# A metaformer block: the expert layer from all eight experts per token to sorted tiles of the two chosen ones

## The chip, the cores and the metric

The kernel runs on one core of a Trainium2 chip. The metric is the time of one execution on the device in microseconds (us). A core has five engines with a queue of instructions each: TensorE (PE, matmuls; its weight loads are listed as PEld), VectorE (DVE), ScalarE (ACT), GpSimd (POOL) and SyncE (SP, which here only issues transfers). They signal each other by semaphores. Results of PE go to PSUM, here eight banks of 128 partitions x 512 float32 numbers, and everything else is in SBUF.

## The reference

An image tensor of 8 x 64 x 16 x 16 passes four stages: a deformable convolution, an LSTM over the 256 positions, a second deformable convolution, and a layer of experts. The change is in the last. There are 2048 tokens of 64 channels, 8 experts with 682 hidden numbers each, and each token's result uses its two most probable experts:

```python
logits = flat @ router_w.T
probs = jax.nn.softmax(logits, axis=-1)
topk_probs, topk_idx = jax.lax.top_k(probs, TOP_K)          # TOP_K = 2
topk_probs = topk_probs / (jnp.sum(topk_probs, axis=-1, keepdims=True) + 1e-09)
onehot = jax.nn.one_hot(topk_idx, N_EXPERTS, dtype=flat.dtype)
gates = jnp.einsum('nk,nke->ne', topk_probs, onehot)
h1 = jnp.einsum('nc,ehc->neh', flat, w1)
h3 = jnp.einsum('nc,ehc->neh', flat, w3)
h = jax.nn.silu(h1) * h3
y = jnp.einsum('neh,ech->nec', h, w2)
out = jnp.einsum('ne,nec->nc', gates, y)
```

`flat` is the layer-normalised input; `out` is added to the input.

## The kernel before

The program is written out engine by engine, and the order of each engine's instructions is the order of the code; nothing is scheduled. Between the engines stand waits on semaphores (`wait_ge`).

**Number format.** Where float32 accuracy is wanted at the speed of float16 matmuls, a number is held as a float16 high part and a float16 rest. The tokens stand as `xp`, with the high parts of 64 channels on 64 partitions and the rests on the other 64, so that one matmul with 128 rows takes both. Weights have a high and a rest matrix (`wh`, `wl`; in `w2p` the two are side by side).

**Weights.** They are loaded at the start (L277, L279). During the LSTM, a serial chain of 256 steps, DVE takes the largest absolute value in 56 pieces (`largest_part`, L1201) and then ACT and DVE split the weights into the two parts in pieces of 256 columns (`high_part` L814, `low_part` L1239). Only two of the four pairs of experts fit beside the originals; the other two are stored and fetched again (L290, L296).

**Expert layer.** After the last layer norm PE makes the logits (L588). DVE computes the gates in a chain of small operations (L1388 to L1415), each of which waits for the one before. ACT and POOL split the tokens (L917 to L1000). Then a loop with two passes over 88 units runs, 176 units in all. A unit is 128 hidden rows of a pair of experts for 512 tokens:

- PE, `first` (L604, L605): four matmuls 128x512, for h1 and h3 with the two parts of the weights.
- ACT: SiLU of h1 (L932). DVE: the product with h3 into `hid` (L1443). ACT: the high part `hh` (L928). POOL: the rest `hl` (L1007).
- PE, `second` (L619), three units later: eight matmuls 128x128 with `hh` and `hl` as the stationary side; in 16 of the units they are 256 columns wide.
- DVE, `gather` (L1427): after eleven units the results of 512 tokens are multiplied by the gates and added to `acc`.

After the loop DVE adds the halves (L1454), PE transposes (L634), DVE adds to the input (L1458), SP stores the output (L301).

Of the kernel before, what the change touches and what calls it, by code (L numbers as in the profile page):

```python
# [22 lines left out]
I32 = mybir.dt.int32  # L23
ALU = mybir.AluOpType
# [4 lines left out]
T = H * W  # L29
# [34 lines left out]
SPLIT = (POWER + 16, POWER + 30 + 2 * PAIRK)  # L64
# [7 lines left out]
MLAG = 3  # L72
MR = 4
# [5 lines left out]
NCH = 4  # L79
CH = B * T // NCH  # L80
JJ = CH // 128

def build(nc, x, consts, conv_w, conv_b, sample_w, bn, lstm_u, lstm_v, lstm_b, router, w13, w2, out):
    with ExitStack() as ctx:
# [6 lines left out]
        bank = [ctx.enter_context(nc.psum_tensor(f"bank{i}", [P, 512], F32)) for i in range(8)]  # L92
# [54 lines left out]
        w13s = sb("w13s", [P, PAIRS, 2 * PH])  # L147
        wh = [sb(f"wh{q}", [P, 2 * PH], F16) for q in range(2)]
        wl = [sb(f"wl{q}", [P, 2 * PH], F16) for q in range(2)]
        w2f = sb("w2f", [P, PAIRS, W2B, C])  # L150
        w2p = [sb(f"w2p{q}", [P, W2B, 2, C], F16) for q in range(2)]
        hid = sb("hid", [P, MR, 512])

        def over(t, at, shape, dt=F32):
# [14 lines left out]
        xp = over(st0, 0, [P, 2 * COLS], F16)  # L170
        silu = over(st0, 1024, [P, 1024]).rearrange("p (u n) -> p u n", u=2)
        acc = over(st1, 0, [P, 2048]).rearrange("p (j h n) -> p j h n", j=8, h=2)
        slo = hid[:, 0:SR // 2, :].rearrange("p a b -> p (a b)").bitcast(F16) \
            .rearrange("p (s k n) -> p s k n", s=SR, k=TG)
        hh = zw[0][:, :, :, :, :].rearrange("p a b c d -> p (a b c d)")[:, 0:MR * 512] \
            .rearrange("p (u n) -> p u n", u=MR)
        hl = zw[1][:, :, :, :, :].rearrange("p a b c d -> p (a b c d)")[:, 0:MR * 512] \
            .rearrange("p (u n) -> p u n", u=MR)
        gt = xc[:, :].rearrange("p (k g e) -> p k g e", k=8, e=E)
        small = spare[:, 0:128].rearrange("p (k g) -> p k g", k=8)  # L180
        g1 = spare[:, 128:256].rearrange("p (j h e) -> p j h e", j=8, h=2)
        ge = spare[:, 256:320].rearrange("p (q j h k) -> p q j h k", q=2, j=8, h=2)
# [17 lines left out]
        for l in range(4):  # L200
            for n in ("mean", "xc", "sq", "var", "sd", "rs", "rb", "rt", "xn"):
                if l != 2 or n not in ("rs", "rb", "rt"):
                    s(f"n{l}_{n}")
        for n in ("ld_const", "ld_mean", "ld_x", "ld_conv", "ld_lstm", "ld_w13", "ld_late", "ld_w2",
                  "zero", "bn_a", "bn_d",
                  "c_max", "c_tr", "c_pow", "c_bc", "c_scale",
                  "w_part", "w_max", "w_tr", "w_pow", "w_bc", "w_scale", "w_fac", "w_high", "w_split", "w_stored", "l_scaled",
                  "l_gi", "l_o", "l_act", "l_oact", "l_c", "l_tc", "l_h", "l_hc", "l_up", "l_res", "l_init", "l_zero", "r_half", "r_seed", "r_newton",
                  "e_pads", "e_conv", "e_om", "e_turn", "e_omt", "e_sig", "e_dist", "e_far", "e_tents", "e_tent",
                  "m_w0", "m_w1", "m_high", "m_scaled", "m_parts", "m_log", "m_max", "m_exp", "m_sm", "m_ge",  # L210
                  "m_h", "m_silu", "m_hid", "m_hh", "m_hl", "m_zero", "m_y", "m_acc", "m_sum", "m_tr",
# [3 lines left out]

# [36 lines left out]

        block = ctx.enter_context(nc.Block())
# [3 lines left out]
        def _(sp):  # L258
# [16 lines left out]
            for e in range(PAIRS):  # L275
                for hf in range(2):
                    sp.dma_start(w13s[hf * C:hf * C + C, e, :], w13[e]).then_inc(s("ld_w13"), 16)  # L277
            for e in range(PAIRS):
                sp.dma_start(w2f[:, e, :, :], w2[e]).then_inc(s("ld_w2"), 16)  # L279

            def parts(q):
                kept = w13s[:, 2 + q, :].bitcast(F16).rearrange("p (k n) -> p k n", k=2)
                kept2 = w2f[:, 2 + q, :, :].rearrange("p a c -> p (a c)").bitcast(F16)
                used2 = w2p[q][:, :, :, :].rearrange("p a k c -> p (a k c)")
                return ((kept[:, 0, :], wh[q][:, :]), (kept[:, 1, :], wl[q][:, :]), (kept2, used2))

            for q in range(2):
                sp.wait_ge(s("w_split"), q + 1)
                for kept, used in parts(q):
# [1250 lines left out]
```

## Time and profile before

| | us |
|---|---|
| three runs of the kernel | 954.67, 957.54, 958.70; median 957.54 |
| span of the profiled execution, first to last instruction | 952.8 |
| LSTM, 145.7 to 559.4 | 413.7 |
| second convolution, to about 670 | 110 |
| layer norm, router and token split, to 689.3 | 19 |
| expert loop, 689.3 to 943.4 | 254.1 |
| tail, to 952.8 | 9.4 |

The profiled execution has no time of its own beside its span; the span is 4.7 us under the median of the runs. The table of slices of the page has each engine's busy share in fortieths of the span. The expert loop is slices 29 to 39: there PE has mostly 9, ACT and POOL 8, DVE 6 and 7, and TensorE's granted clock stands at 9. A span of an instruction goes from its start to its modelled end; since matmuls are pipelined, the distance from one start to the next says what a matmul costs its engine.

### The profile page before, as it was taken

The page shows a single profiled execution, that of the slowest core. Times are in us where ns is not written, and L with a number is a line of the kernel's source. Part 1 is how long each engine was busy: PE and PEld are TensorE (multiplying, and loading weights), DVE is VectorE, ACT ScalarE, POOL GpSimd, SP SyncE. Part 2 cuts the span into 40 slices and gives each one's busy share as a digit, 9 for nine tenths or more (in the row PEclk, how much of TensorE's full clock was granted, in tenths as well). Part 3 has the DMA queues.
Part 4 walks back from the last instruction along what each step waited for, and adds up shares of the span by engine and source line. Part 5 has one row for each costly group of instructions (what it writes and reads, how often), then busy time and mean ns, then how long its engine had stood idle before and what let it go on. Part 6 is the DMA issues. An engine that isn't in the chain of part 4 may idle for free.

```text
span 952.8 us, 18695 instructions
## 1 busy us (share of the span) xinstructions
PE 800.3 (84%) x6356; PEld 594.2 (62%) x6356; DVE 570.5 (60%) x1752; ACT 556.2 (58%) x1664; POOL 366.6 (38%) x297
## 2 busy tenths in 40 slices
PE   5899987777777776789988768999689999899995
PEld 3587875555655555566666547889446666466663
DVE  3888854556456466334344346887457667467765
ACT  3676752333355365334444355777478888588884
POOL 0878620000000000003000007874268888588884
PEclk7999995555555555555555556999689999899998
DMA  9700000000001100000000000000000100200001
GB/s 224 175 2 1 2 1 1 1 1 1 0 1 78 78 1 1 1 0 1 1 1 1 1 1 1 2 1 2 1 1 2 59 21 2 80 1 2 2 1 23
DMA packets 5860, 18.54 MB, mean 19 GB/s; under 512 B 1093, under 2 KB 2822, under 8 KB 5254
## 3 DMA queue, kind: packets, MB, share of 16 engines
q1 hardware_dynamic: 5478, 17.21, 6.2%
q8 instruction: 52, 0.85, 0.4%
q14 instruction: 42, 0.34, 0.1%
q10 hardware_dynamic: 288, 0.13, 0.1%
HBM read 9.47 MB, written 0.52 MB: 10 GB/s over the span
## 4 chain that ended last, share of the span: by engine, by line
PE 41%; POOL 22%; DVE 13%; issue 11%; ACT 11%; DVEq 1%; POOLq 1%; DMA 0%; SPq 0%; ACTq 0%
POOL zw L1007 21%; PE bank L558 10%; PE bank L383 6%; PE bank L560 6%; PE bank L400 6%; DVE bank L1320 5%; PE bank L348 4%; DVE hr L1324 4%; ACT bank L885 4%; ACT bank L889 4%; PE bank L524 2%; PE bank L370 1%; DVE hid L1089 1%; PE bank L315 1%; PE bank L413 1%
## 5 line engine op out<-in xcount | busy, mean ns | idle before, releaser
L1007 POOL TENSOR_TENSOR zw<-hid,zw 128x512 f16<-128x512 f32 x176 | 203.9, 1159 | 49.3 <-ACT zw L928 38.9
L558 PE MATMUL bank<-hr,lv 64*64 64x8 f32 x512 | 97.0, 261 | 98.8 <-DVE hr L1324 98.4
L966 POOL TENSOR_TENSOR st<-tent,tentx 128x768 f32<-128x768 f32 x72 | 112.2, 1589 | 173.3 <-DVE tentx L1081 123.8
L1443 DVE SCALAR_TENSOR_TENSOR hid<-bank,wsc,st 128x512 f32<-128x512 f32 x176 | 131.9, 750 | 76.0 <-ACT st L932 70.1
L558 PEld LDWEIGHTS bank<-hr,lv 64*64 64x64 f32 x512 | 72.8, 201 | 158.4 <-DVE hr L1324 158.2
L885 ACT ACTIVATE bank<-bank 64x16 f32<-64x16 f32 x256 | 39.2, 153 | 196.8 <-PE bank L560 196.5
L604 PE MATMUL bank<-st,wh 128*128 128x512 f16 x352 | 136.9, 389 | 11.5 <-POOL st L1000 5.4
L932 ACT ACTIVATE st<-bank,wsc 128x512 f32<-128x512 f32 x176 | 120.9, 687 | 39.8 <-PE bank L605 22.0
L605 PE MATMUL bank<-st,wl 128*128 128x512 f16 x352 | 136.8, 389 | 0.0
L966 POOL TENSOR_TENSOR st<-sq 128x768 f32<-128x768 f32 x9 | 13.2, 1498 | 309.3 <-DVE sq L1309 308.5
L1320 DVE TENSOR_TENSOR_SCAN bank<-bank,scan_add 64x24 f32<-64x24 f32 x256 | 52.9, 207 | 127.8 <-ACT bank L885 127.5
L619 PEld LDWEIGHTS bank<-w2p,zw 128*128 128x128 f16 x1408 | 96.8, 98 | 45.4 <-POOL zw L1007 4.1
L619 PE MATMUL bank<-w2p,zw 128*128 128x128 f16 (+1 forms) x1408 | 114.2, 224 | 3.0 <-POOL zw L1007 3.0
L717 ACT ACTIVATE shi<-bank 128x512 f16<-128x512 f32 x144 | 85.4, 596 | 52.2 <-PE bank L383 51.0
L1089 DVE SCALAR_TENSOR_TENSOR hid<-bank,shi 128x512 f16<-128x512 f32 x144 | 96.1, 686 | 31.0 <-ACT shi L717 29.8
L928 ACT CAST zw<-hid 128x512 f16<-128x512 f32 x176 | 106.9, 608 | 4.1 <-DVE hid L1443 4.1
L383 PE MATMUL bank<-ident,st 128*128 128x128 f32 x576 | 91.7, 283 | 1.7 <-DVE hid L1089 1.4
L560 PE MATMUL bank<-hr,lv 64*64 64x8 f32 x512 | 91.6, 251 | 0.0
L562 PE MATMUL bank<-hr,lv 64*64 64x8 f32 x512 | 91.6, 251 | 0.0
L560 PEld LDWEIGHTS bank<-hr,lv 64*64 64x64 f32 x512 | 84.7, 224 | 0.0
L562 PEld LDWEIGHTS bank<-hr,lv 64*64 64x64 f32 x512 | 84.4, 223 | 0.0
L1324 DVE SCALAR_TENSOR_TENSOR hr<-tog,bank 64x8 f32<-64x8 f32 x256 | 39.4, 154 | 72.7 <-ACT bank L889 72.7
(184 smaller groups left out, 1340.4 us busy)
## 6 DMA issues: line engine op xcount, KB each, us to landing
w13s<-w SPq DMA_DIRECT2D x8, 704.0 KB, 17.9
w2f<-w SPq DMA_DIRECT2D x4, 384.0 KB, 25.4
w13s<-wh SPq DMA_DIRECT2D x2, 704.0 KB, 3.7
w13s<-wl SPq DMA_DIRECT2D x2, 704.0 KB, 5.0
wh<-w13s SPq DMA_DIRECT2D x2, 704.0 KB, 3.9
wl<-w13s SPq DMA_DIRECT2D x2, 704.0 KB, 5.1
w2f<-w2p SPq DMA_DIRECT2D x2, 384.0 KB, 4.9
w2p<-w2f SPq DMA_DIRECT2D x2, 384.0 KB, 5.7
```

The source lines that it names most:

```text
L383: mm = nc.tensor.transpose(bank[3 + g % RING][:, k * 128:k * 128 + 128], st[m % 2][:, t, tap, half * 128:half * 128 + 128], ident[:, :])
L558: nc.tensor.matmul(both[:, 0, t, :], lv[:, C:2 * C], prev, start=False, stop=True, skip_group_check=True)
L560: nc.tensor.matmul(both[:, 1, t, :], lv[:, 0:C], prev, start=False, stop=True, skip_group_check=True).then_inc(s("l_gi"), 1)
L562: nc.tensor.matmul(go, lv[:, 2 * C:3 * C], prev, start=False, stop=True, skip_group_check=True).then_inc(s("l_o"), 1)
L604: nc.tensor.matmul(bk[:, :], wh[q][:, col:col + 128], xp[:, tok], start=True, stop=False)
L605: nc.tensor.matmul(bk[:, :], wl[q][:, col:col + 128], xp[:, tok], start=False, stop=True)\
L619: mm = nc.tensor.matmul(bank[4 + 2 * (g % 2) + j // 2][:, lo:lo + n], part[:, u % MR, j * 128:j * 128 + 128], rhs, start=(t == 0 and j % 2 ...
L928: nc.scalar.copy(hh[:, u % MR, :], hid[:, u % MR, :]).then_inc(s("m_hh"), 1)
L932: nc.scalar.activation(silu[:, u % 2, :], bank[u % 2][:, :], ACT.Silu, scale=wsc[:, 4:5])\
L966: nc.gpsimd.tensor_tensor(st[p][:, t, k:k + KG, :].rearrange("p k (y x) -> p k y x", x=16), ty, tx, ALU.mult)\
L1007: nc.gpsimd.tensor_tensor(hl[:, u % MR, :], hid[:, u % MR, :], hh[:, u % MR, :], ALU.subtract)\
L1443: nc.vector.scalar_tensor_tensor(out=hid[:, u % MR, :], in0=bank[2 + u % 2][:, :], scalar=wsc[:, 5:6], in1=silu[:, u % 2, :], op0=ALU.mult ...
```

## The change

Only the chosen experts are computed. The 4096 pairs of a token and an expert are sorted by expert, and each expert's pairs are padded to tiles of 128. With 8 experts, 39 tiles hold every possible outcome, and the program always runs 39.

1. **Routing** (DVE, L1537 to L1591). The two best experts are found from the logits; a scan over each partition's tokens and two matmuls with constant matrices (`ones_p`, `upper`, L672, L673) give each pair its place in the sorted order; 33 comparisons build two selection matrices (`tsel`, `lsel`), and 32 matmuls (L679) turn them into a list of tokens by tile and lane. From it come `xidx` (what to fetch), `yidx` (where results go) and `etab` (the expert of each tile). The gates are computed after that.
2. **Tokens** are transposed (L666), split by ACT and POOL and written to memory by one transfer (`xrows`, L364).
3. **Tiles.** For each tile POOL issues an indirect transfer that fetches 128 rows of 256 bytes (L1157), PE transposes them (L692), ACT copies them (`xts`), PE does `first` with the tokens as the stationary side and the weights as the moving side, 341 columns at a time (L705). ACT takes SiLU of 682 columns, DVE the product, PE transposes the product in six blocks (L716), ACT makes the high part, DVE the rest, and PE does `second` (L729) with 12 matmuls of 128 columns. DVE adds the two halves of the result (L1627), and POOL issues an indirect transfer that spreads the 128 rows in memory (L1164).
4. **Weight addresses.** PE loads the tile's expert from `etab` into a register (L685) and computes the addresses of the weights from it. All weights now stay in SBUF in both parts; the stores and fetches L290 and L296 go away, and the loads are 52 transfers in place of 12. The split during the LSTM has 64 pieces of at most 228 columns in place of 56 of 256.
5. **Tail.** SP waits for all the spread rows, reads them back in two transfers (L369), and DVE multiplies by the gates and adds.

The core of the diff:

```diff
-W13K = 2 * PAIRS * PH // CHUNK
-W2K = PAIRS * W2B * C // CHUNK
-PAIRK = 2 * PH // CHUNK + W2B * C // CHUNK
+W13K = 44
+W2K = 12
+HCUT = [0, 228, 456, 684, 912, 1140, EW]
+PAIRK = 16
+TILE = 128
+NT = (2 * B * T + E * (TILE - 1)) // TILE
+AHEAD = 4
...
@@ tensor
-                        nc.tensor.matmul(bk[:, :], wh[q][:, col:col + 128], xp[:, tok], start=True, stop=False)
-                        nc.tensor.matmul(bk[:, :], wl[q][:, col:col + 128], xp[:, tok], start=False, stop=True)\
...
+            def expert(t):
+                return pe.value_load(etab[0:1, t:t + 1], min_val=0, max_val=E - 1)
+            def turn_tokens(t):
+                pe.wait_ge(s(f"m_g{t % AHEAD}"), 16 * (t // AHEAD + 1))
+                if t > 0:
+                    pe.wait_ge(s("m_xts"), t)
+                nc.tensor.transpose(bank[4][:, 0:64].bitcast(F16), xg[:, t, :], ident16[:, :])\
+                    .then_inc(s("m_xtp"), 1)
+            def first(t, e):
+                n = HID // 2
+                pe.wait_ge(s("m_xts"), t + 1)
+                for m in range(2):
+                    if t > 0:
+                        pe.wait_ge(s(("m_silu", "m_hid")[m]), t)
+                    for half in range(2):
+                        for part in range(2):
+                            at = 2 * SLOT + part * EW + m * HID + half * n
+                            mm = nc.tensor.matmul(duo[m][:, half * 512:half * 512 + n], xts[:, t % 3, :],
+                                                  w16[:, bass.ds(e * SLOT + at, n)],
+                                                  start=(part == 0), stop=(part == 1))
+                    mm.then_inc(s("m_h"), 1)
+            def turn_hidden(t):
+                pe.wait_ge(s("m_hid"), t + 1)
+                for b in range(EB):
+                    if t > 0 and b % 4 == 0:
+                        pe.wait_ge(s("m_hl"), 2 * t - 1 + b // 4)
+                    mm = nc.tensor.transpose(bank[6 + b // 4][:, b % 4 * 128:b % 4 * 128 + 128],
+                                             htok[:, t % 2, b * 128:b * 128 + 128], ident[:, :])
...
+            for t in range(NT + 2):
+                if t < NT:
+                    first(t, owners[t])
+                    if t + 1 < NT:
+                        owners.append(expert(t + 1))
+                        turn_tokens(t + 1)
+                if 1 <= t <= NT:
+                    turn_hidden(t - 1)
+                if t >= 2:
+                    second(t - 2, owners[t - 2])
@@ gpsimd
-                    nc.gpsimd.tensor_tensor(hl[:, u % MR, :], hid[:, u % MR, :], hh[:, u % MR, :], ALU.subtract)\
-                        .then_inc(s("m_hl"), 1)
+            def fetch(t):
+                if t >= AHEAD:
+                    gp.wait_ge(s("m_xtp"), t - AHEAD + 1)
+                gp.indirect_dma_start(xg[:, t, :], None, xrows[:, :],
+                                      bass.IndirectOffsetOnAxis(ap=xidx[:, t:t + 1], axis=0))\
+                    .then_inc(s(f"m_g{t % AHEAD}"), 16)
+            def spread(t):
+                gp.wait_ge(s("m_ys"), t + 1)
+                gp.indirect_dma_start(yrows[:, :], bass.IndirectOffsetOnAxis(ap=yidx[:, t:t + 1], axis=0),
+                                      ybuf[:, t, :], None).then_inc(s("m_rows"), 16)
+            for t in range(AHEAD):
+                fetch(t)
+            gp.wait_ge(s("m_idx"), 2)
+            for t in range(NT):
+                if t + AHEAD < NT:
+                    fetch(t + AHEAD)
+                spread(t)
@@ vector
+            for t in range(NT + 2):
+                if t < NT:
+                    gated(t)
+                if 1 <= t <= NT:
+                    low(t - 1)
+                if t >= 2:
+                    rows_out(t - 2)
```

PE's queue in the middle of the expert loop before, one unit, with what each instruction waits for (names are those of the tensors; `st` holds the tokens `xp`, `zw` the parts `hh` and `hl`):

```order
L600 REGISTER_ALU
L604 MATMUL bank<-st,wh 128x512 [waits m_hid]
L605 MATMUL bank<-st,wl 128x512
L604 MATMUL bank<-st,wh 128x512
L605 MATMUL bank<-st,wl 128x512
L619 MATMUL bank<-w2p,zw 128x128 [waits m_hl]
L619 MATMUL bank<-w2p,zw 128x128 x7
```

And now, in a tile, from the last matmul of `first` (`st` holds the rows `xg` and `xts`, `hid` the product `htok`, `w2s` the weights of `second`; ISA is a register instruction):

```order
L705 MATMUL duo<-w13s,st 128x341
L685 TENSOR_LOAD etab
L685 ISA x2
L692 MATMUL bank<-ident,st 128x128 [waits m_xts,m_g0]
L716 MATMUL bank<-ident,hid 128x128 [waits m_hl,m_hid]
L716 MATMUL bank<-ident,hid 128x128 x3
L716 MATMUL bank<-ident,hid 128x128 [waits m_hl]
L716 MATMUL bank<-ident,hid 128x128
L729 ISA [waits m_hl,m_ys]
L729 MATMUL bank<-w2s,zw 128x128 x2
```

Each pair of matmuls of `second` and each matmul of `first` has a register instruction ahead of it, and the transposition of the next tile's rows, which waits for a transfer (`m_g0`), stands ahead of the hidden transpositions of the tile before.

POOL's queue at the start of the expert loop before:

```order
L990 MEMSET st 128x2048 [waits c1_out_ps]
L1000 TENSOR_TENSOR st<-sq,st 64x1024 [waits m_scaled,m_high,m_zero]
L1000 TENSOR_TENSOR st<-sq,st 64x1024 [waits m_parts,m_scaled,m_high]
L1004 UNCONDITIONAL_BRANCH [waits m_parts]
L1004 ISA
L1007 TENSOR_TENSOR zw<-hid,zw 128x512 [waits m_hh]
```

And now:

```order
L1143 MEMSET hid 128x2x86 [waits c1_sz_done,c1_out_ps]
L1148 TENSOR_TENSOR st<-sq,st 128x8x64 [waits m_high] x2
L1157 DMA st<-xrows,xidx 128x128 [waits m_idx,m_xrow]
L1157 DMA st<-xrows,xidx 128x128 x3
L1157 DMA st<-xrows,xidx 128x128 [waits m_xtp,m_idx]
L1164 DMA yrows<-st,yidx 9216x64 [waits m_ys]
L1157 DMA st<-xrows,xidx 128x128 [waits m_xtp]
```

POOL no longer computes in the loop; it issues a fetch and a spread for each tile, in turn, and the spread of tile t (which waits for its result, `m_ys`) stands ahead of the fetch of tile t + 5.

## Rows read from the trace of the kernel before

**Rows 1.** The page's chain that ended last, by engine and by line.
```profile
PE 41%; POOL 22%; DVE 13%; issue 11%; ACT 11%; DVEq 1%; POOLq 1%; DMA 0%; SPq 0%; ACTq 0%
POOL zw L1007 21%; PE bank L558 10%; PE bank L383 6%; PE bank L560 6%; PE bank L400 6%; DVE bank L1320 5%; PE bank L348 4%; DVE hr L1324 4%; ACT bank L885 4%; ACT bank L889 4%; PE bank L524 2%; PE bank L370 1%; DVE hid L1089 1%; PE bank L315 1%; PE bank L413 1%
```
**Rows 2.** Stages: start:end, length, busy us by engine, clock, DMA share, GB/s.
```profile
145.70:559.40 413.70, 314.85 (x1969) 244.63 (x1968) 206.30 (x1101) 174.12 (x937) 8.84 (x6) 0.50 0.03 10
680.00:695.00 15.00, 7.53 (x26) 4.54 (x25) 10.38 (x27) 6.13 (x7) 4.23 (x2) 0.50 0.00 0
689.30:943.36 254.06, 244.75 (x2112) 153.62 (x2112) 167.72 (x317) 210.60 (x352) 203.86 (x176) 0.97 0.04 16
```
**Rows 3.** Groups of instructions in 700 to 800: busy us, mean ns, idle before.
```profile
L1007 POOL TENSOR_TENSOR zw<-hid,zw 128x512 f16<-128x512 f32 x75 | 86.9, 1159 | 14.4 <-ACT zw L928 9.8
L1443 DVE SCALAR_TENSOR_TENSOR hid<-bank,wsc,st 128x512 f32<-128x512 f32 x75 | 56.3, 750 | 32.8 <-ACT st L932 31.5 <-issue 0.4
L932 ACT ACTIVATE st<-bank,wsc 128x512 f32<-128x512 f32 x75 | 51.5, 687 | 11.3 <-PE bank L605 3.5
L928 ACT CAST zw<-hid 128x512 f16<-128x512 f32 x74 | 45.0, 607 | 0.0
```
**Rows 4.** Timeline, PE, one unit: start, duration, instruction.
```profile
703.36 0.38 PE L604 MATMUL bank<-st,wh 128*128 128x512 f16 x1
...
704.22 0.61 PE L619 MATMUL bank<-w2p,zw 128*128 128x128 f16 x8
...
704.67 0.38 PE L604 MATMUL bank<-st,wh 128*128 128x512 f16 x1
```
**Rows 5.** Timeline of the second convolution: transposes, and what reads them.
```profile
663.19 0.60 PE L383 MATMUL bank<-ident,st 128*128 128x128 f32 x4
...
663.58 0.69 DVE L1089 SCALAR_TENSOR_TENSOR hid<-bank,shi 128x512 f16<-128x512 f32 x1 [0.20 <-ACT shi L717]
663.63 0.22 PE L400 MATMUL bank<-zw,shi 128*128 128x128 f16 x1
```
**Rows 6.** Router: one row of the timeline, then groups by shape.
```profile
683.98 0.29 DVE L1388 TENSOR_REDUCE spare<-bank 128x16 f32<-128x128 f32 x1 [2.83 <-PE bank L588]
...
L1396 DVE TENSOR_TENSOR xc<-xc,spare 128x128 f32<-128x128 f32 x1 | 1.9, 1932 | 0.0
L1415 DVE TENSOR_SCALAR spare<-spare,wsc 128x128 f32<-128x128 f32 x1 | 0.3, 286 | 0.0
L1407 DVE SCALAR_TENSOR_TENSOR spare<-spare 128x16 f32<-128x16 f32 x1 | 0.2, 174 | 0.0
L1000 POOL TENSOR_TENSOR st<-sq,st 64x1024 f16<-64x1024 f32 x2 | 4.2, 2116 | 12.0 <-ACT sq L920 11.8 <-POOL st L1000 0.2
```
**Rows 7.** Transfers: issues, KB each, median us from issue to landing; one issue.
```profile
xs<-x SPq DMA_DIRECT2D x2, 256.0 KB, 4.5
out<-xs SPq DMA_DIRECT2D x4, 128.0 KB, 2.5
mean_w<-consts ACTq DMA_DIRECT2D x1, 64.0 KB, 1.9
...
5.09 0.43 SPq L269 DMA_DIRECT2D convw<-conv_w  x1
```
**Rows 8.** The chain in order of time: POOL's queue between two units.
```profile
937.20 0.03 POOLq L1006
```
**Rows 9.** Timeline, DVE, two LSTM steps with a piece of the split.
```profile
275.05 0.21 DVE L1320 TENSOR_TENSOR_SCAN bank<-bank,scan_add 64x24 f32<-64x24 f32 x1 [0.22 <-ACT bank L885]
...
275.95 0.47 DVE L1239 SCALAR_TENSOR_TENSOR wl<-w13s,wsc,wh 128x256 f16<-128x256 f32 x1
276.64 0.21 DVE L1320 TENSOR_TENSOR_SCAN bank<-bank,scan_add 64x24 f32<-64x24 f32 x1 [0.22 <-ACT bank L885]
```
**Rows 10.** Timeline of the tail.
```profile
943.36 2.29 DVE L1427 SCALAR_TENSOR_TENSOR st<-bank,spare,st 128x128 f32<-128x128 f32 x8 [3.21 <-PE bank L619]
...
947.12 1.29 DVE L1458 TENSOR_TENSOR xs<-xs,bank 128x512 f32<-128x512 f32 x2 [0.15 <-PE bank L634]
```

More of the change, by code:

```diff
@@ L184, in place @@
+        tiles, ends, start_c = [rk[:, 8 * k:8 * k + 8] for k in range(3)]
+        spot, away, tile_n, lane, gate = [rk[:, 32 * k:32 * k + 32].rearrange("p (k g) -> p k g", k=2)
+                                          for k in range(1, 6)]
+        bits = rk[:, 192:192 + NP40 // 2].bitcast(F16)
+        raw = rk[:, 224:224 + NP40].bitcast(I32)
+        passed = spare[0:1, 0:NP40 * E].rearrange("p (t e) -> p t e", e=E)
+        owner = rk[0:1, 264:264 + NP40]
         def place(p, g):
@@ new lines, in _ @@
+            for j in range(8):
+                mm = nc.tensor.transpose(bank[4 + j // 4][:, j % 4 * 128:j % 4 * 128 + 128],
+                                         xn[:, j * 128:j * 128 + 128], ident[:, :])
+                if j % 4 == 3:
+                    mm.then_inc(s("m_xps"), 1)
+            pe.wait_ge(s("m_rank"), 1)
+            last = counts[:, :, 15]
+            nc.tensor.matmul(bank[7][:, 0:E], ones_p[:, :], last, start=True, stop=True, skip_group_check=True)
+            nc.tensor.matmul(bank[7][:, E:2 * E], upper[:, :], last, start=False, stop=True, skip_group_check=True)\
+                .then_inc(s("m_tot"), 1)
@@ new lines, in _ @@
+            pe.wait_ge(s("m_tsel"), 1)
+            for c in range(32):
+                if c % 8 == 0:
+                    pe.wait_ge(s("m_lane"), c // 8 + 1)
+                mm = nc.tensor.matmul(bank[7][:, 64:64 + NP40], lsel[:, c, :], tsel[:, c, :],
+                                      start=(c == 0), stop=(c == 31), skip_group_check=True)
+            mm.then_inc(s("m_code"), 1)
+            def expert(t):
+                return pe.value_load(etab[0:1, t:t + 1], min_val=0, max_val=E - 1)
@@ new lines, in second @@
+            def second(t, e):
+                if t > 0:
+                    pe.wait_ge(s("m_ys"), t)
+                for b in range(EB):
+                    if b % 4 == 0:
+                        pe.wait_ge(s("m_hl"), 2 * t + 1 + b // 4)
+                    for part in (hh, hl):
+                        mm = nc.tensor.matmul(bank[5][:, 0:2 * C],
+                                              part[:, t % 3, b * 128:b * 128 + 128],
+                                              w216[:, bass.ds(e * HP + (2 * HP + b * 128), 128)],
+                                              start=(b == 0 and part is hh), stop=(b == EB - 1 and part is hl),
+                                              skip_group_check=True)
+                mm.then_inc(s("m_y"), 1)
@@ L903, in _ @@
                     early_tents(image_step(n, 12))
-                for part in range(2):
-                    if SPLIT[part] <= n < SPLIT[part] + 2 * PAIRK:
-                        high_part(2 * PAIRK * part + n - SPLIT[part])
+                if split_piece(n) is not None:
+                    high_part(split_piece(n))
             act.wait_ge(s("l_h"), STEPS + 1)
@@ L939, in _ @@
+            turned_tokens(0)
+            for t in range(NT + 1):
+                if t < NT:
+                    gated(t)
+                if t + 1 < NT:
+                    turned_tokens(t + 1)
+                if t > 0:
+                    high(t - 1)
         @block.gpsimd
@@ L1002, in _ @@
[L1002 to L1008 removed]
+            gp.wait_ge(s("c1_sz_done"), NG * B)
+            nc.gpsimd.memset(htok[:, :, HID:HP], 0.0).then_inc(s("m_zero"), 1)
@@ new lines, in _ @@
+            for c in range(32):
+                k, g = c // 16, c % 16
+                ins = nc.vector.tensor_scalar(lsel[:, c, :], lane_c[:, :], lane[:, k, g:g + 1], code_v[:, c:c + 1],
+                                              ALU.is_equal, ALU.mult)
+                if c % 8 == 7:
+                    ins.then_inc(s("m_lane"), 1)
+            note(nc.vector.tensor_tensor(passed, tile_c[0:1, :].unsqueeze(2).broadcast_to([1, NP40, E]),
+                                         ends[0:1, :].unsqueeze(1).broadcast_to([1, NP40, E]), ALU.is_ge))
```

517 lines of the change are left out of this document (281 added, 236 removed).

## The prediction

> **What bounds the kernel now.** I read the page's chain first: the loop's POOL instruction (L1007) alone is 21% of the span, the largest line [rows 1]. Then the table by stages. The expert loop takes 254.1 of 952.8 us; in it PE is busy 244.8 and POOL 203.9 us, at a granted clock of 0.97, that is, at the 2.4 GHz level nearly throughout [rows 2]. Then the groups within the loop and one unit of the timeline. A 512-column matmul costs PE 0.215 us (four from 703.36 to 704.22) and one of 128 columns 0.056 (eight from 704.22 to 704.67), so a unit is 1.31 us of gapless PE [rows 4]; POOL needs 1.16 and 0.15 between two [rows 3]. The loop is bound by PE and POOL at once: 176 x 1.31 = 231 us, the rest being wide units, the turn of the loop and the start. The LSTM (413.7 us) and the convolutions are not touched but for the pieces of the weight split.
>
> **What goes.** The whole loop and, ahead of it, POOL's two passes over `xp` (L1000, 2.12 us each) [rows 6]. The weight stores and fetches ran beside other work and give nothing.
>
> **The LSTM.** 64 pieces in place of 56, each a little smaller. A step with a DVE piece of 0.47 us goes from 275.05 to 276.64, 1.59 us, with DVE idle 0.22 before the next scan [rows 9]: the piece lies in DVE's slack. Cost 0; without that cover, 8 x 0.47 = 4 us. The 52 loads are issued at 0.43 us each [rows 7], 22 us, under the first convolution, and are needed only in the LSTM: 0.
>
> **Work in a tile.** PE by the rows above: eight matmuls of 341 columns at 0.143 (0.215 x 341/512) = 1.14, one transpose 0.06, six float32 transposes at 0.11 (663.19 to 663.63 for four [rows 5]) = 0.66, twelve of 128 columns = 0.67; together 2.5 us. 39 tiles are 99 us of PE against 231: not a quarter, since tokens are padded and the hidden numbers must be transposed. DVE: product of 682 columns 0.95 (0.75 for 512 [rows 3], with the 1.2 ns per column between it and the 0.29 for 128 columns [rows 6]), rests of 512 and 256 columns 0.69 and 0.42 (0.69 [rows 5]), sum of 128 columns 0.29; 2.35. ACT: SiLU 0.9 (0.69 x 682/512), high parts 0.61 and 0.35, tokens 0.3; 2.2 [rows 3]. POOL: two issues, 2P.
>
> **What a tile costs.** No engine is full at these numbers, so I look for the chain that closes on itself. Call P POOL's time for one indirect issue and L the time from its end to landing. The result of tile t is summed (`m_ys`); POOL issues its spread (P), then the fetch of tile t+5 (P), which lands after L. PE transposes that fetch in the middle of tile t+4, and behind it, in order, stand the six transposes of tile t+3 and `second` of t+2, whose sum closes the ring two tiles further on. From the landing: transposes 0.06 + 0.60, `hh` 0.61, `hl` 0.69 + 0.42, last four matmuls of `second` with the tail of the last 0.39, sum 0.29: 3.1 us. So two tiles take 2P + L + 3.1. A second ring needs no transfer: product of tile t starts, PE's transposes, `hh`, both `hl`, sum, next product: 0.66 + 0.61 + 1.11 + 0.29 = 2.7 us.
>
> P is not in this trace. Below, SP's issue of a plain transfer: 0.43 [rows 7]. Above, the longest POOL instruction here over 128 or 64 partitions, 2.12 [rows 6]. I take 1.2, near the pass over 128 partitions (1.16 [rows 3]), since 128 rows must be addressed. L: the smallest timed transfer lands 1.9 after the start of its issue, so 1.5 after its end; the longest row here is 4.5 [rows 7]. A fetch is 32 KB: I take 2.0. Then T = (2.4 + 2.0 + 3.1)/2 = 3.75 us per tile, 39 tiles 146 us.
>
> The Trainium skill (SBUF — State Buffer, "A bandwidth-pool intuition that's wrong") tells of a GpSimd-issued transfer that took 0.62 us alone and 3.1 beside a DVE copy in a two-port mode, because GpSimd could not write its descriptors. Its section "Who interferes with whom" excepts tensor_tensor and reductions, the kinds DVE runs in the tiles, so by the page P is not lengthened; no row here has such an issue, and the price would be that of the slower rival below.
>
> Register instructions: one costs 0.03 on POOL's queue [rows 8], and PE's own between units is not to be seen in the 1.31 [rows 4]. 14 in a tile, each behind matmuls of 0.11 or more: 0. The load of `etab` from SBUF is not in the trace: between 0.03 (one register instruction) and 1.9 (the shortest memory transfer). It stands behind the four matmuls (0.57) of the second half of `first` and ahead of a wait for a transfer, so I cost it at 0; its upper end, 1.3 us past that cover, would lengthen only the second ring, to 4.0. The Trainium skill (DMA: Bandwidth & Descriptors, "Latency and other measured facts") puts a floor of about 0.6 us under it; by that figure the sum stays as it is.
>
> **Ahead of the tiles.** DVE starts at 683.98 [rows 6]. 13 operations of 128 columns at 0.29 + 0.03: 4.2. POOL splits tokens at that time, and a DVE operation of 0.29 took 1.93 beside POOL [rows 6]: 1.5 more; 689.7. Two counting matmuls 0.6; eight small operations at 0.17 + 0.03, one of 128 and two of 256 columns: 2.8; `tsel`, 1280 columns at 1.03 ns: 1.5; 694.6. `lsel`, 32 operations of 128 float16 columns, between 0.17 and 0.32 each [rows 6]; I take 0.2, 6.4 in all (10.2 at the upper end); 701.0. The last eight of 32 matmuls at the low clock and three small operations: 1.6; first fetch at 702.6. The write of the tokens to memory ends at about 692, beside this.
>
> **Tiles.** First rows 3.2 later, 705.8; 39 x 3.75 to 852.1; the last results 3.1, their spread 3.2: 858.4. The clock stands at 0.50 from 680 to 695 [rows 2], and it will at the first tiles: PE work of 2.5 doubles for about one tile, 3 us: 861.4.
>
> **Tail.** Reading back 1 MB: 4.5 by the two loads of `xs` (smaller, so this is low by 1 or 2) [rows 7]; gates 1.2 and sum 0.69 for each half, 3.8; transposes 0.6, addition 0.65; then from the end of the last addition at 948.41 to the end of the span 4.4 [rows 10]. Span 875.4, against 952.8: 77 less. The median lies 4.7 over the span; 957.5 - 77.4 = 880. All but the 39T is 734 in time.
>
> **Rivals.**
> *The fetches are hidden.* If P is 0.43 and L 1.5, the first ring falls to 2.7, where the second stands; with 0.5 of waits T is 3.2. For it: AHEAD is 4, and POOL has nothing else. Against it: the spread stands ahead of the fetch in POOL's queue. Time 734 + 39 x 3.2 = 859, at 2.7 839.
> *PE stays at the low level, or the transfers are long.* In a tile PE works 2.5 of 3.75 us, and the LSTM, with PE listed busy 315 of 414, ran all through at 0.50 [rows 2]. At 1.2 GHz a tile is 4.9 us of PE (0.28 per 341 columns, 0.11 per 128, transposes 0.2). Against it: a PE that is full at 1.2 GHz is what the loop before was at its start, and its clock rose. Time 734 - 3 + 191 = 922. With P at 2.1 T is 4.65 and the time 915; with L at 4.5, 929.
> The Trainium skill (TensorE: Matmul & The Clock Gate, "What's actually happening") says that the low rate is the default and that activity releases it; the trace agrees with 0.50 in 680 to 695 and 0.97 in the loop, and by that rule a tile pace with a third of idle could fall either way: 880 or 922.
> *Slower than before: POOL's issue is the bound.* Two issues a tile, so T is at least 2P. The kernel is slower once 39T exceeds 224, T 5.7, P 2.9 us. At P = 3.3 T is 6.6 and the time 991. For it: 128 separately addressed rows, in software. Against it: the longest POOL row here is 2.12.
>
> **How the numbers follow.** Forecast, T 3.4 to 4.3, 867 to 902: 0.50. Fetches hidden, 839 to 863: 0.20. Low clock or long transfers, 905 to 948: 0.24. POOL-bound past the old time: 0.06. The range 845 to 928 leaves out some of the first rival's low end, the top of the second and the last. Within 0.5% is what a measurement here cannot tell from no change; only the last case comes near: faster 0.94, same 0.01, slower 0.05.
>
> **What would show it.** PE: distance from one group of L705 to the next, 3.75 us, at clock 1.0 with PE waiting at L692 for the fetch; waits named for a transfer mean the first ring, for L1621 or L1627 the second. POOL: P in the queue's rows at L1157 and L1164; landing in the transfer list. First L1157 at 702.6 less what the LSTM moved; last L1164 to the end of the span 17 us. An LSTM other than 414 +-2 us breaks the claim on the pieces. A P over 2 or a clock under 0.9 in the tiles breaks the forecast.

## The result, and the profile after

The changed kernel took 868.76 us (median of 4 runs, 866.73 to 870.40), the kernel before 956.46 in the same session (4 runs, 954.67 to 958.70): a ratio of 0.9078, with an interval of 0.9054 to 0.9101. Forecast were 880, range 845 to 928. The profiled execution took 870.40 us, its span is 868.5.

The stages of the changed kernel, in the columns of [rows 2] (start:end, length, then busy us of PE, its weight loads, DVE, ACT and POOL with the number of instructions, TensorE's granted clock, DMA share, GB/s):

```profile
145.70:560.00 414.30, 316.28 (x1978) 246.01 (x1979) 206.11 (x1107) 174.96 (x942) 8.89 (x6) 0.50 0.00 1
684.00:705.90 21.90, 4.99 (x46) 4.04 (x46) 19.46 (x68) 3.66 (x6) 2.31 (x2) 0.50 0.06 24
705.90:710.00 4.10, 0.96 (x4) 0.59 (x5) 1.79 (x7) 0.27 (x1) 3.16 (x4) 0.50 0.08 16
...
760.00:800.00 40.00, 31.10 (x307) 23.97 (x306) 23.96 (x45) 21.80 (x45) 22.70 (x24) 1.00 0.09 20
852.70:868.50 15.80, 2.23 (x8) 1.43 (x8) 5.03 (x6) 0.00 (x0) 0.01 (x1) 0.50 0.35 102
```

The LSTM is where it was, 414.3 against 413.7 us. The 254 us of the old loop have become 145.4 us of tiles, from the first rows at 708.5 to the last spread's landing at 853.9. The routing with its indices takes 21.5 us to the first fetch, where the old one had the loop running 5 us after the router's first row, and the tail is 14.6 where it was 9.4. In the tiles no engine is full: PE, the busiest, has 31.1 of 40 us, at the full clock.

What the engines wait for from 725 to 840, some 32 tiles (engine, line waited for: us in total, times, longest):

```profile
POOL yrows L1164 <- DVE st L1627: 41.9, 32, 2.9
PEld bank L692 <- DMA st<-xrows,xidx: 34.2, 28, 2.7
DVE zw L1621 <- ACT zw L1064: 30.4, 31, 2.6
```

PE waits for the fetched rows, its weight loads in 28 of 32 tiles (the matmuls themselves in 23); POOL waits in every tile for the sum, and only behind that does it issue the fetch that PE will wait for. The chain of waits from one fetch in it to the next, a round of two tiles, and on into the tile behind (start, us, what):

```profile
753.87 2.40 DMA st<-xrows,xidx
756.27 0.05 issue
756.32 0.23 PE bank L692
756.55 0.71 PE bank L716 x6
...
758.77 0.21 DVE st L1627
758.98 0.27 issue
759.25 0.98 POOL yrows L1164
760.23 0.30 issue
760.54 2.85 DMA st<-xrows,xidx
763.39 0.05 issue
...
765.05 1.16 PE duo L705 x8
766.21 0.23 issue
766.45 0.22 PE bank L692
```

The round is 6.67 us, from 753.87 to 760.54. Between the transposes and the sum (L1627) the chain names PE's next blocks; in the timeline DVE works through the rests there, which stand ahead of the sum in its queue and begin when ACT's high part is done:

```profile
757.75 1.02 DVE L1621 TENSOR_TENSOR zw<-bank,zw 128x512 f16<-128x512 f32 x2 [1.49 <-ACT zw L1064]
```

The next fetch takes from 760.54, start of the issue, to 763.39, rows landed: 2.85 us, of which the issue is 0.97. From the landing PE's blocks (transposes L716, second layer L729, first layer L705) stand without a gap until 766.21. There is one of 0.23, at the place where the expert of the next tile is loaded into a register, and the transpose behind it (L692) takes 0.22 where a transpose of this size costs 0.06. Neither mattered here, as e2_static shows; later they do.

The page's group of the spreads, which answers to [rows 3] for POOL (busy us, mean ns, idle before):

```profile
L1164 POOL DMA_INDIRECT yrows<-st,yidx x39 | 38.4, 985 | 58.9 <-DVE st L1627 58.9
```

The same line by itself (duration ns min/median/max, first and last start us):

```profile
L1164 POOL DMA_INDIRECT yrows<-st,yidx x39: 967/985/1003, 719.3 to 851.7; - x39
```

(851.7 - 719.3) / 38 is 3.48 us per tile. This measure, first to last start of the spreads, is the "pace" below. It includes the last tiles, where the fetches run out and which go faster.

### The profile page after: what moved, and what is told of

Its sections match the earlier page's. It is cut to its first block, busy times and chain, and to the rows that moved or that the text cites. A ratio compares the mean times of both kernels' runs of the same rounds, so it can differ in the third digit from the quotient of the medians.

```text
span 868.5 us, 16095 instructions
## 1 busy us (share of the span) xinstructions
PE 672.0 (77%) x5341; PEld 528.9 (61%) x5341; DVE 508.4 (59%) x1661; ACT 422.1 (49%) x1477; POOL 237.2 (27%) x209
## 3 DMA queue, kind: packets, MB, share of 16 engines
q0 software_dynamic: 2496, 2.56, 1.4%
## 4 chain that ended last, share of the span: by engine, by line
PE 47%; DVE 20%; ACT 11%; issue 10%; DMA 7%; POOL 2%; DVEq 1%; SPq 1%; POOLq 0%; ACTq 0%
DMA st<-xrows,xidx 6%; DVE bank L1472 6%; PE duo L632 5%; PE bank L632 5%; PE bank L474 4%; DVE hr L1476 4%; PE duo L422 4%; ACT duo L1002 4%; ACT bank L1006 4%; PE duo L634 3%; PE bank L634 3%; PE bank L457 3%; PE duo L705 3%; DVE hid L1254 2%; PE duo L598 2%
## 5 line engine op out<-in xcount | busy, mean ns | idle before, releaser
L1472 DVE TENSOR_TENSOR_SCAN bank<-duo,scan_add 64x24 f32<-64x24 f32 x256 | 52.9, 207 | 126.5 <-ACT duo L1002 126.1
L636 PE MATMUL bank<-hr,lv 64*64 64x8 f32 x512 | 91.6, 251 | 0.0
L632 PE MATMUL bank<-hr,lv 64*64 64x8 f32 x256 | 48.6, 261 | 51.9 <-DVE hr L1476 51.8
L632 PEld LDWEIGHTS bank<-hr,lv 64*64 64x64 f32 x256 | 36.5, 202 | 81.6 <-DVE hr L1476 81.6
L632 PE MATMUL duo<-hr,lv 64*64 64x8 f32 x256 | 48.6, 261 | 46.7 <-DVE hr L1476 46.4
L636 PEld LDWEIGHTS bank<-hr,lv 64*64 64x64 f32 x512 | 84.4, 223 | 0.0
L474 PE MATMUL bank<-zw,shi 128*128 128x128 f16 x576 | 78.9, 219 | 0.8 <-DVE hid L1254 0.6
L474 PE MATMUL bank<-zw,hid 128*128 128x128 f16 x576 | 78.9, 219 | 0.0
L1621 DVE TENSOR_TENSOR zw<-bank,zw 128x512 f16<-128x512 f32 x78 | 39.9, 553 | 34.9 <-ACT zw L1064 34.9
L474 PEld LDWEIGHTS bank<-zw,shi 128*128 128x128 f16 x576 | 56.3, 98 | 1.8 <-DVE hid L1254 1.5
L474 PEld LDWEIGHTS bank<-zw,hid 128*128 128x128 f16 x576 | 56.3, 98 | 1.5
L705 PE MATMUL duo<-w13s,st 128*128 x312 | 55.1, 322 | 0.9 <-ACT st L1047 0.9
L1164 POOL DMA_INDIRECT yrows<-st,yidx x39 | 38.4, 985 | 58.9 <-DVE st L1627 58.9
```

Of the source, the lines that this page charges most:

```text
L474: mm = nc.tensor.matmul(bank[6][:, lo:lo + 2 * C], part[:, place(p, h), k, :], zw[p][:, half, tap, :, :].rearrange("p k c -> p (k c)"), st ...
L632: nc.tensor.matmul(both[:, 0, t, :], lv[:, C:2 * C], prev, start=False, stop=True, skip_group_check=True)
L636: nc.tensor.matmul(go, lv[:, 2 * C:3 * C], prev, start=False, stop=True, skip_group_check=True).then_inc(s("l_o"), 1)
L705: mm = nc.tensor.matmul(duo[m][:, half * 512:half * 512 + n], xts[:, t % 3, :], w16[:, bass.ds(e * SLOT + at, n)], start=(part == 0), stop ...
L1472: nc.vector.tensor_tensor_scan(cell[:, :, :].rearrange("p b k -> p (b k)"), gates, scan_add[:, :, :].rearrange("p b k -> p (b k)"), 0.0, A ...
```

## The experiments

All stand beside runs of the kernel before on the same chip; ratios are to that. The changed kernel's own is 0.9078. The pace is read from each run's profile.

| run | us, median (runs) | ratio, 95% interval | pace, us |
|---|---|---|---|
| changed kernel | 868.76 (4) | 0.9078, 0.9054 to 0.9101 | 3.48 |
| e1_swap | 851.05 (4) | 0.8883, 0.8858 to 0.8907 | 2.93 |
| e2_static | 869.93 (4) | 0.9068, 0.9045 to 0.9090 | 3.49 |
| e3_pad | 885.09 (4) | 0.9231, 0.9210 to 0.9253 | 3.87 |
| e4_ahead6 | 848.35 (4) | 0.8864, 0.8830 to 0.8897 | 2.93 |
| e5_swap_static | 831.94 (5) | 0.8704, 0.8685 to 0.8723 | 2.53 |
| e6_swap_pad | 859.96 (4) | 0.8999, 0.8979 to 0.9020 | 3.28 |
| e7_later | 846.56 (5) | 0.8865, 0.8842 to 0.8889 | 2.93 |
| e8_hoist | 849.04 (5) | 0.8892, 0.8874 to 0.8911 | 2.94 |
| e10_multi | 846.21 (5) | 0.8837, 0.8816 to 0.8859 | 2.82 |
| e11_loadonly | 834.86 (4) | 0.8720, 0.8699 to 0.8740 | 2.55 |
| e9_best | 845.89 (5) | 0.8840, 0.8821 to 0.8859 | 2.88 |
| e12_nocheck | 832.57 (5) | 0.8697, 0.8672 to 0.8721 | 2.56 |

### What sets the pace: the ring through POOL

**e1_swap**

```diff
-            for t in range(NT):
+            for t in range(NT + 1):
                 if t + AHEAD < NT:
                     fetch(t + AHEAD)
-                spread(t)
+                if t > 0:
+                    spread(t - 1)
```

> POOL issues the fetch of a tile ahead of the spread of an earlier one (fetch t+4, then spread t-1) instead of behind it, so a late spread no longer holds a fetch. Theory A: the pace of 3.60 us per tile is a ring over two tiles: spread 1.29, fetch 1.29, landing 1.5, then 3.1 of PE, ACT and DVE work to the next sum. With the swap the ring runs over three tiles (2.4 per tile), and the work of PE in its own order, 3.0 us per tile with the gap at the loading of the register, binds: 39 x 0.6 = 20 to 23 us less than the changed kernel, 846 to 850. Rival B, the two issues on POOL or the register load set the pace by themselves: within 5 us of 869. Rival C, the fetches are then hidden wholly and PE reaches its 2.6 us of array work: 830.

851.05 us, 1 above the range that I gave for theory A, with a pace of 2.93 for its 3.0: theory A. The chain of waits no longer leaves PE:

```profile
758.89 1.17 PE duo L705 x8
760.06 0.17 issue
760.23 0.22 PE bank L692
760.44 0.76 PE bank L716 x6
761.20 0.67 PE bank L729 x12
```

No transfer is named any more. One tile is 2.98 us: 2.60 for L705, L716 and L729, and the gap and the slow transpose at L692. The order of two issues on POOL is worth 17.7 us.

**e2_static.** `return pe.value_load(etab[0:1, t:t + 1], ...)` becomes `return t * E // NT`.

> The expert of a tile is a constant of the program instead of a number loaded from the table, so PE's load, its wait and the register instructions on the weights' addresses go. It leaves out that the expert is the one that the router chose. Theory A (the ring through fetch and spread sets the pace, and the load does not stand in it): 0 to 4 us less than 869, and PE waits longer for the fetch in place of the load. Rival B (the load and the addresses in registers set the pace): 0.4 us x 39 = 15 us less, 854, and up to 30 less.

869.93 us, pace 3.49: no difference. While the ring holds PE, the load and all the address arithmetic are free.

**e3_pad.** Ahead of `fetch(t + AHEAD)` stands `nc.gpsimd.memset(xn[:, :], 0.0)`.

> A fill of 128x1024 float32 on POOL, about 0.9 to 1.0 us, ahead of each of the 35 fetches that run beside the tiles. Theory A: it stands in the ring of two tiles, so each tile is longer by half of it: 35 x 0.47 = 16 us over 869, 883 to 888. Rival B (PE's work or the register load sets the pace and POOL has slack): 869, within 3 us. Rival D (POOL's own queue is full): 35 x 0.95 = 33 over, 902.

885.09 us, 16.3 more; the fill took 0.97 us, so half of it times 35 is 17.0. That half is the mark of a ring that closes every second tile; it excludes both POOL with slack and POOL full.

**e4_ahead6.** `AHEAD = 4` becomes `AHEAD = 6`.

> Six fetches ahead in place of four (AHEAD = 6, two more semaphores), with the order on POOL as it was. Theory A: the ring now closes over four tiles (6.0 / 4 = 1.8 us) and cannot bind; the pace is PE's 3.0 as with the swap, less 2 x 1.3 us only if the two more fetches ahead of the first tile delay it: 846 to 851. Rival E (it is the time of the transfers themselves, fetch against spread on one queue, not their order): as 869, within 4 us, here and with the swap.

848.35 us, pace 2.93. POOL's order is as in the changed kernel, and the gain is that of the swap (the intervals overlap). So the cost was that the ring was short, not what the transfers take; rival E falls.

**e6_swap_pad.** The swap and the fill.

> The swap, and the same fill of 128x1024 on POOL ahead of each fetch. Theory A: the ring runs over three tiles now, (2.6 + 1.5 + 3.1 + 0.95) / 3 = 2.7 us, and lies under PE's 2.98, so the fill costs nothing: 849 to 854. Rival (POOL's time is itself on the path, as the 16 us of the fill in the other order might also be read): 867, and over 3 tiles a third of it, 862.

859.96 us, 9 over the swap (11 by the ratios), pace 3.28: my expectation of no cost was wrong. The chain shows why:

```profile
755.45 0.97 POOL st L1157
756.43 0.30 issue
756.73 0.99 POOL yrows L1164
757.72 0.97 POOL xn L1173
758.69 0.17 issue
```

POOL is full: 0.97 + 0.30 + 0.99 + 0.97 + 0.17 = 3.40 us, and that is over PE's 2.98. (The pace of 3.28 is lower, since the last four tiles have no fetch and no fill.) I had worked out the ring and not added up the engine. The gap is 0.17 behind a fill and 0.30 behind an issue, so without the fill POOL's sum is 0.97 + 0.30 + 0.99 + 0.30 = 2.56 us, the next bound below PE's.

### What holds PE once the ring is gone

**e5_swap_static.** The swap and the constant expert.

> The swap on POOL, and the expert of a tile as a constant (it leaves out that the expert is the one that the router chose). With the swap PE is the bound: 2.98 us per tile, of which 2.60 are matmuls and transposes; the rest is a gap of about 0.2 at the place where the register is loaded and a transpose of 0.22 behind it. Theory A: the load was hidden as long as the ring held PE, and is now on the path; without it 2.65 to 2.75 per tile, 9 to 13 us under the swap's 851: 838 to 842. Rival: the gap belongs to the wait for the fetched rows and not to the load: 851, within 2.

831.94 us, 19 under the swap (17 by the ratios), more than I expected. The same stretch as above:

```profile
758.82 1.17 PE duo L705 x8
759.98 0.06 PE bank L692
760.04 0.66 PE bank L716 x6
760.70 0.67 PE bank L729 x12
```

1.17 + 0.06 + 0.66 + 0.67 is 2.56 us a tile without a gap. So 0.42 us a tile came with the expert in a register: the gap, and the transposes that followed it at 0.22 and 0.76 instead of 0.06 and 0.66. It cost nothing in e2_static and 17 to 19 us here. POOL is full in this version too, at the same 2.57 us a tile: each of its instructions from 769 to 790 starts 0.30 or 0.31 behind the one before it, and three tiles take 7.70 us (773.11 to 780.81).

```profile
773.11 0.99 POOL L1164 DMA_INDIRECT yrows<-st,yidx  x1 [0.30 <-DVE st L1628]
```

**e8_hoist.** The load moves behind `turn_hidden(t - 1)`.

> The swap, and the load of the next tile's expert stands behind the six transposes of the hidden numbers (0.76 us of queued work) instead of behind the first layer's matmuls. Theory A: if the gap of 0.2 and the slow first transpose come from the load's time, it is now covered by the transposes in part or wholly: 2.7 to 2.85 us per tile, 5 to 11 us under the swap: 840 to 846. Rival 1: a load empties PE's queue wherever it stands, and the gap only moves: 851, within 2. Rival 2: the gap is the wait for the fetched rows: also 851, and the gap stays ahead of the transpose of the tokens.

849.04 us, pace 2.94: the same as the swap. The gap is gone from L692 and has been spread over other lines:

```profile
756.26 1.30 PE duo L705 x8
757.56 0.05 PE bank L692
...
758.36 0.97 PE bank L729 x12
```

The twelve matmuls of L729 take 0.97 instead of 0.67 and the eight of L705 1.30 instead of 1.17. A tile is as long wherever the load stands. That speaks for a limit on PE's whole instruction stream, not for one wait.

**e10_multi.** One load for four experts (`values_load_multi_w_load_instructions(etab[0:1, t:t + 4], ...)`, at every fourth tile), on top of the swap.

> The swap, and one load brings the experts of four tiles into four registers: 10 loads in place of 39; the register instructions on the addresses, 14 in a tile, stay as they are. Theory L: each load stops PE's instruction stream for a time that the few matmuls queued behind it don't cover, 0.42 us, wherever it stands; three tiles of four then take 2.56 us and the fourth 3.0 to 3.1: mean 2.68, 39 x 0.3 = 11.5 us under the swap's 851: 838 to 842. Rival S: the 14 register instructions on addresses are what makes PE's stream late; then the loads don't matter and the time stays at 849 to 851.

846.21 us, pace 2.82; a third of what theory L expected, more than rival S. The trace has both halves of the answer:

```profile
754.61 1.16 PE duo L707 x8
755.77 0.92 issue
756.69 0.22 PE bank L694
756.90 0.76 PE bank L718 x6
...
759.49 0.06 PE bank L694
...
762.05 0.06 PE bank L694
```

A tile without a load (759.49 to 762.05) is 2.56 us, with all 14 address instructions in it: they alone are hidden. A load of four costs 1.2 us at once here (gap 0.92, transposes 0.26 longer); over the nine loads within the tiles the gap is 0.92 to 1.25, mean 1.03, so 1.3 against the 0.42 of a load of one. The cost grows with the number of values, and fewer loads save little.

**e11_loadonly.** The swap with `first(t, t * E // NT)` and `second(t - 2, (t - 2) * E // NT)`, the load kept.

> The swap, with the load of every tile's expert kept and its value not used: the addresses are constants of the program, so the matmuls have no register instructions between them (it leaves out that the expert is the one that the router chose). Theory L (the load costs): 2.95 to 3.0 us per tile, 846 to 851. Rival S (the address instructions cost): 2.56 per tile, 832. In between (the load's time is made longer by the instructions behind it, since the stream must catch up): 2.75 to 2.85, 840 to 844.

834.86 us, pace 2.55: the load, with all that stands behind it, is hidden as well when the address instructions are gone. Each of the two fits beside the array's 2.56 us, their sum doesn't. (POOL is full here as well, at 2.57 us.) This time is near what I gave for rival S (832); e10 says that it is not the address instructions by themselves either.

**e9_best.** The swap; loads of eight; POOL's subtractions later (e7); `xidx` and `yidx` formed ahead of `etab`; and, for the read back, a semaphore for each half:

```diff
-rows[:, q * 1024:q * 1024 + 1024]).then_inc(s("m_yld"), 16)
+rows[:, q * 1024:q * 1024 + 1024]).then_inc(s(f"m_yld{q}"), 16)
...
-                dve.wait_ge(s("m_yld"), 32)
+                dve.wait_ge(s(f"m_yld{q}"), 16)
```

> The swap; eight experts per load, 5 loads in all; POOL's subtractions after the count; the indices formed ahead of the table of experts; and a semaphore of its own for each half that is read back, so that DVE starts on the first half when that has landed. Theory: 39 x (2.98 - 2.62) = 14 us from the loads, 0.9 and 1.0 from the two edits ahead of the tiles, 0 to 1.9 from the halves: 832 to 836. If the halves land together, 834 to 836; if the loads don't matter (rival S) 847 to 849.

845.89 us, pace 2.88, outside what I expected: the loads of eight cost as much as those of four. The idle time ahead of the transpose of the tokens, from the timeline, at two of the four loads within the tiles (2.46 and 2.42 at the others; the idle time stands in brackets):

```profile
730.08 0.22 PE L694 MATMUL bank<-ident,st 128*128 128x128 f16 x1 [2.42 <-issue]
753.16 0.27 PE L694 MATMUL bank<-ident,st 128*128 128x128 f16 x1 [2.34 <-issue]
```

1.03 for four and 2.41 for eight, both means: 0.35 us for each further value. For each value the program issues two register instructions behind the load, a compare and the check that the value lies within 0 to 7.

> As the version with all edits, but with four experts per load, and without the two register instructions (compare, check of bounds 0 to 7) behind the load for each value; the values are clamped to 0..7 where the table is made. So far the gap at a load grew with its values: 0.42 us a tile for one, 1.2 for four, near 2.8 for eight, about 0.34 per value. Theory C (the two instructions per value cost this, the load itself little): no gap left, 2.56 to 2.62 us per tile, 39 x 0.37 = 14.5 under the swap's 851, and 1 to 3 from the edits ahead of the tiles and behind them: 832 to 836. Rival (bringing a value into a register costs it, checked or not): the gap of 1.2 at every fourth tile stays, 2.86 per tile: 842 to 846. If the load with its round trip still costs once per four tiles, 0.5 to 0.9 of the 1.2: 837 to 841.

832.57 us, pace 2.56: theory C. PE is now full, as with constant experts, here from 760 to 800 in the columns of the stages:

```profile
760.00:800.00 40.00, 40.00 (x424) 33.42 (x422) 33.24 (x63) 28.48 (x63) 30.42 (x32) 1.00 0.12 28
```

Its chain of waits has the transpose behind the load's place at 0.06 again:

```profile
756.76 0.06 PE bank L695
```

The four loaded values cost nothing that the trace can show. POOL is all but full too (32 instructions, 30.42 us busy, with 0.30 or more between two), so nothing that is taken from PE alone can shorten a tile further. This version is 4% faster than the changed kernel (0.8697 against 0.9078) and computes the same.

### Ahead of the tiles

**e7_later.** The swap, and `gp.wait_ge(s("m_rank"), 1)` ahead of POOL's two subtractions.

> The swap, and POOL's two subtractions for the low parts of the tokens wait until DVE has counted the choices (m_rank), so they no longer run beside DVE's operations of 128 columns. Theory: two DVE operations took 1.13 us instead of 0.29 beside POOL; they go back to 0.29, the subtractions then run beside DVE's wait for PE and small operations, and the tokens' write to memory still ends before the indices are there: the first fetch starts 1.2 to 1.7 us sooner, time 849.5 to 850. Rival: the collision only moves to the operations behind it (two of 128 and 256 columns): first fetch within 0.5 of before; a second: the later write of the tokens holds the first fetch.

In the changed kernel these two ran from 686.54, and two operations of DVE beside them took 1.13 and 1.12 us where their like take 0.29:

```profile
686.54 2.31 POOL L1148 TENSOR_TENSOR st<-sq,st 128x512 f16<-128x512 f32 x2 [13.39 <-ACT st L1035]
686.71 1.13 DVE L1545 TENSOR_TENSOR xc<-xc,spare 128x128 f32<-128x128 f32 x1
...
687.87 1.12 DVE L1546 TENSOR_TENSOR xc<-xc,rank_c 128x128 f32<-128x128 f32 x1
```

Moved later, the first of them fell into DVE's wait for PE and cost nothing; the second stretched one operation of eight columns, which took 0.17 in the changed kernel (group of DVE, the mean in ns behind the comma):

```profile
L1561 DVE TENSOR_SCALAR rk<-rk 128x8 f32<-128x8 f32 x1 | 1.0, 986 | 0.0
```

From the router's first operation to the first fetch it is 20.6 us instead of 21.5: half of the collision is back, half has moved. The median can't tell it from the swap's (the ratios' intervals overlap); the trace can. The two other edits of e9_best and e12_nocheck, read the same way: the indices ahead of the table bring 0.5 more (20.15 us; in e9_best the first tile then waited 0.88 for its eight checked values, in e12_nocheck it didn't); a semaphore for each half brings the tail from the start of the last spread's issue to the end from 16.8 to 15.6.

## Why the prediction was right, and where it was off

The profiled span is 6.9 us under the forecast's 875.4. The other 4.3 of the 11.2 between 880 and 868.76 are no step of the kernel: I set 4.7 us between the span and the median (the runs show 1.9 between a span and its own execution), and the profiled execution is 1.6 slower than the median.

- **What goes, and the LSTM.** Right: 414.3 us; the 64 pieces cost less than 1.
- **The ring.** Right, and the reason for the result: spread, fetch, landing, transposes, rests, sum, over two tiles; e3_pad shows the two, e1_swap and e4_ahead6 that it binds. In the chain from 720.65 to 834.81, 32 tiles, eleven rounds go from fetch to fetch over two tiles, in 6.66 to 8.48 us, mean 7.08 for 7.5 (most of the others take in a third tile, which PE sets alone). Each term was a little high: the two issues with the gap between them 2.25 for 2.4 (0.98 + 0.30 + 0.97); L from the end of the issue 1.43 to 3.24, mean 1.84, for 2.0; from the landing to the next spread 2.98 for 3.1. In the last I had left out the 0.27 between the sum and the issue, and counted 0.39 for matmuls of `second` that run under DVE's rests. Those 32 tiles take 3.57 us each for 3.75, 5.8 us less in all. The last six, as the fetches run out, take 3.04 each ((851.74 - 833.52) / 6), where I had let the ring hold them too: 4.3 less. Together that is the 10.2 (38 x 0.27) by which the tiles were shorter, the largest error of the sum. That L came out near 2.0 is in part luck, since the trace had no gather.
- **Register instructions and load at 0.** The number was right for this kernel (e2_static), the reason wrong. I set each register instruction behind a matmul and found each covered; but the stream as a whole, 14 for the addresses and the load with its check, makes a tile longer than the array's work by 0.42 (e1_swap against e5_swap_static). The ring hid it. The bound that I gave, "only the second ring, to 4.0", was the wrong mechanism too: e8_hoist moved the load and nothing changed.
- **Rival "the fetches are hidden", 839 to 863.** It did not occur, because the spread stood ahead of the fetch, as was written against it. With them hidden (e1_swap) the pace is 2.93 and the time 851; its 3.2 of "waits" had no mechanism.
- **Rival "low clock".** PE idle for over a fifth of the time kept the clock at 1.00, but for two places, where fetches took 3.91 and 3.67 us to land and PE idled for them, 2.38 us ahead of 745.47 and 2.14 ahead of 838.53. (An idle time of 2.06 ahead of 817.12 left it at 1.00.) In the chain of waits at the first, the eight matmuls of L705 took 2.28 us instead of 1.16:

```profile
741.51 3.91 DMA st<-xrows,xidx
...
747.14 2.28 PE duo L705 x8
```

and in the columns of the stages the clock stood at 0.50, the lower of its two levels:

```profile
748.00:750.00 2.00, 2.00 (x10) 1.39 (x9) 0.62 (x2) 1.09 (x2) 1.29 (x2) 0.50 0.02 6
```

  The price was some 1.6 us of PE's work at each of the two, not 40. At the first tiles the clock stood at 0.50, as forecast. That activity releases the full rate is what the Trainium skill states (TensorE: Matmul & The Clock Gate, "What's actually happening"); the trace agrees, 0.50 from 705.9 to 710 and 1.00 from 760 to 800.
- **Rival "POOL-bound past the old time".** An issue took 0.94 to 1.00 us in every tile (1.18 for the very first), also beside DVE's product, a SCALAR_TENSOR_TENSOR, which the prediction's list of DVE's kinds in the tiles had left out, and P with the gap to the next was 1.29, not 2.9. But two of them, 2.57 a tile, are as much as PE's 2.56: with the ring and the checks gone, both are full.
- **Ahead of the tiles.** First fetch at 705.9 for 702.6: 3.3 us late. 0.5 is the router's start; 1.2 the operations from there to `tsel`, 10.3 for 9.1; 0.7 the 32 operations of `lsel` at 0.223 for 0.2; 0.2 the last matmuls and small operations; and 0.76 passes between the last index and POOL's first issue, which I had not counted. Then the first rows came in 2.6 for 3.2.
- **Collision of DVE and POOL.** Forecast 1.5 from [rows 6], measured 1.7.
- **Tail.** Right within 0.6: 14.6 behind the last landing for 14.0; the two halves took 4.9 for 4.5.

Sum against the forecast span: +3.3 - 0.6 - 10.2 + 0.6 = -6.9.

What stays open: how long the load, the compare, the check and an address instruction each take in PE's stream. The runs give only sums: addresses alone fit into 2.56 us, load and check alone too, both together need 2.98, and each checked value more in one load 0.35. e12_nocheck took out the compare and the check together; which of them it is was not tried, nor was a single unchecked load for each tile. Nor do they show how far PE's work could be cut to advantage, since POOL has no time left in e5_swap_static, e11_loadonly and e12_nocheck.

## What to carry to other kernels

When a result and a request share one queue, issue the request first, and count over how many iterations the ring closes: here the order of two issues (17.7 us) or two more buffers (20.4) was worth more than 0.97 us in every fetch (16.3, e3_pad). A cost of zero "because it is hidden" holds for the present bound only; sum each engine's instruction stream too, register instructions and checks among them, since the next change lays it bare. And add up the engine that gets the extra work before trusting a ring (e6_swap_pad), with the gaps between its instructions: POOL's two issues are 1.96 us busy a tile and fill 2.57.

## What the hardware showed that I had not expected

- An indirect transfer of 128 rows holds POOL for 0.94 to 1.00 us and the next one for 0.30 more, for a fetch as for a spread; a fetch lands 2.3 to 4.2 us after its issue starts, median 2.5.
- Loading experts into PE's registers with a check of bounds costs 0.35 us for each further value of a load when the stream is full, and nothing that can be seen without the compare and the check, which was tried for loads of four.
- While POOL passes over 128x512, one operation of DVE from SBUF is held until the pass is over, at both sizes seen: 128 columns 1.13 us instead of 0.29, eight columns 0.99 instead of 0.17; one operation for each pass. Whether an operation that reads PSUM is held too is not shown: the two near a pass in e7_later (0.27 for 128 columns, 0.17 for eight) started 0.17 ahead of it and at the seam of two passes.
- Of four equal idle times of PE in e9_best (2.34 to 2.46 us), two left the transpose behind them at 0.22 us and two at 0.27; behind the one at 753.16 the granted clock was 0.50 to 756.1; behind the one at 778.01 it stayed at 1.00:

```profile
753.20:754.80 1.60, 1.60 (x9) 1.52 (x10) 0.00 (x0) 0.60 (x2) 0.09 (x1) 0.50 0.13 21
```
